# A two-layer adaLN kernel on one core: setup's waits moved into attention, a router in three stages, one product of the slots on VectorE

## The reference

```python
mod = (silu(c) @ wmod).reshape(16, 6, 1, -1)       # sa, ca, ga, sb, cb, gb
ga = (2 * (ga >= 0) - 1) * max(abs(ga), 0.25)       # gb likewise
h = layernorm(x) * (1 + ca) + sa
x = x + ga * mixer(h)       # layer 0: 8-head retention; layer 1: selective scan
h = layernorm(x) * (1 + cb) + sb
x = x + gb * experts(h)     # layer 0: each expert takes its 64 best tokens; layer 1: below

# experts of layer 1
var = mean(x * x, -1)
h = rms_weight * (x * rsqrt(var + 1e-6))
scores = softmax(h @ gate_w.T)                      # 8 experts
top_w, top_i = top_k(scores, 2); top_w /= sum(top_w)
a, g = h @ w1[e].T, h @ w3[e].T
return x + sum over the two e of top_w * ((silu(a) * g) @ w2[e].T)
```

## Time and profile before

| what | us |
|---|---|
| median of 3 runs (lowest, highest) | 1334.08 (1330.05, 1343.19) |
| the profiled execution | 1332.48 |
| its span, first to last instruction | 1330.7 |
| busy in the span: PE, DVE, ACT, POOL | 1047.5, 843.9, 667.6, 621.0 |
| setup to attention's first statistics | 0 to 28.47 |
| router, from its first statistics | 933.89 to 1011.70 |
| slots | 1011.70 to 1049.9 |
| MoE | 1049.9 to 1289.9 |

### The profile page before, as it was taken

The page is one execution under the profiler, slowest core; times in us unless marked ns, Lnnn a source line. Parts: engine busy times, 40 slices in busy tenths (PEclk is TensorE's granted clock), DMA queues, the critical chain, the costliest instruction groups (busy, mean ns, idle before and its releaser), DMA issues. The chain is left out here.

```text
span 1330.7 us, 24554 instructions
## 1 busy us (share of the span) xinstructions
PE 1047.5 (79%) x7112; PEld 826.9 (62%) x7113; DVE 843.9 (63%) x1612; ACT 667.6 (50%) x1488; POOL 621.0 (47%) x922
## 2 busy tenths in 40 slices
PE   1899964899986889998888999861563499999950
PEld 1577752377685788888778888861342277777640
DVE  2566646422234899999999999990577543433327
ACT  1454521433404888888888888840341233333320
POOL 1000001200012899999999999960001456666630
PEclk9988856899997999999999999995665599999985
DMA  6000000375512000000000000005110011111125
GB/s 200 1 1 1 1 1 6 80 167 135 124 33 76 13 13 21 15 12 12 12 12 12 23 13 12 12 1 185 29 32 16 10 39 43 43 41 43 40 80 167
DMA packets 51468, 59.07 MB, mean 44 GB/s; under 512 B 5401, under 2 KB 45282, under 8 KB 50034
## 3 DMA queue, kind: packets, MB, share of 16 engines
q1 hardware_dynamic: 42322, 41.50, 11.8%
q0 software_dynamic: 4608, 9.45, 2.5%
q10 hardware_dynamic: 4496, 7.60, 1.7%
HBM read 49.32 MB, written 9.21 MB: 44 GB/s over the span
## 5 line engine op out<-in xcount | busy, mean ns | idle before, releaser
L1180 DVE TENSOR_TENSOR_SCAN s_hs<-s_dA,bank 128x1024 f32<-128x1024 f32 x128 | 291.6, 2278 | 10.3 <-PE bank L1577 9.6
L1437 POOL TENSOR_SCALAR s_dbuT<-s_dtuT,s_BT 128x256 f32<-128x256 f32 x512 | 241.0, 491 | 11.5 <-POOL s_bc L1375 5.4
L1298 ACT ACTIVATE s_dA<-s_dt,aneg 128x255 f32<-128x255 f32 x512 | 211.7, 495 | 0.2
L1577 PE MATMUL bank<-const,s_dbuT 128*128 128x128 f32 x1024 | 136.1, 277 | 3.1 <-POOL s_dbuT L1437 3.1
L1191 DVE TENSOR_TENSOR s_hc<-s_hs,bank 128x1024 f32<-128x1024 f32 (+1 forms) x128 | 130.3, 1018 | 5.8 <-PE bank L1565 1.1
L1595 PE MATMUL bank<-const,s_hc 128*128 128x128 f32 x832 | 113.9, 276 | 20.9 <-DVE s_hc L1191 20.9
L2102 PE MATMUL bank<-w,x_xT 128*128 x288 | 125.2, 557 | 5.8 <-issue 4.0
L1577 PEld LDWEIGHTS bank<-const,s_dbuT 128*128 128x128 f32 x1024 | 117.0, 143 | 6.3 <-POOL s_dbuT L1437 3.6
L1595 PEld LDWEIGHTS bank<-const,s_hc 128*128 128x128 f32 x832 | 95.5, 142 | 24.7 <-DVE s_hc L1191 24.7
L2140 ACT ACTIVATE x_a<-bank 128x448 f32<-128x448 f32 x72 | 39.1, 544 | 138.5 <-PE bank L2102 138.5
L2062 POOL DMA_INDIRECT x_xg<-hf_rows,x_src x72 | 69.7, 968 | 70.1 <-DVE x_src L2160 40.1
(11 more groups left out here) (298 smaller groups left out, 2198.0 us busy)
## 6 DMA issues: line engine op xcount, KB each, us to landing
xn<-prob_d SPq DMA_DIRECT2D x16, 512.0 KB, 7.5
s_Crow<-C_rows SPq DMA_DIRECT2D x48, 128.0 KB, 2.8
w<-in_w SPq DMA_DIRECT2D x16, 256.0 KB, 3.1
o_yr<-y_rows SPq DMA_DIRECT2D x8, 512.0 KB, 3.9
w<-in_w ACTq DMA_DIRECT2D x1, 3584.0 KB, 13.2
x_res<-in_x SPq DMA_DIRECT2D x4, 512.0 KB
gate<-gates_d SPq DMA_DIRECT2D x2, 1024.0 KB, 5.6
spread<-place_d SPq DMA_DIRECT2D x8, 256.0 KB, 5.8
```

The source lines that it names most:

```text
L1180: dve.tensor_tensor_scan(flat(hs[:, j % 2]), flat(dA[:, j % RING]), bDbu[j % 2], 0.0, ALU.mult, ALU.add).then_inc(S["scanned"], 1)
L1298: ins = act.activation(dA[:, j % RING, h, n, 1:], dt[:, k, h, 1:], ACT.Exp, scale=m.aneg[:, h, 2 * j + n:2 * j + n + 1])
L1437: ins = pool.tensor_scalar(dbuT[:, j % RING, c, n, :], dtuT[:, k, c, :], BT[:, k, c, 2 * j + n:2 * j + n + 1], 1.0, ALU.mult, ALU.mult)
L1577: mm = pe.transpose(out[:, h, n, c * P:(c + 1) * P], dbuT[:, j % RING, c, n, h * P:(h + 1) * P], ident)
```

## The change

- **Setup** ends when the first x load, the front part of `const` (up to `C_T72`, that is without the later tables and the masks), `wq`, `wk`, `wv` and the modulation are there. `wq` to `gn` are issued by ScalarE behind its Silu, and so is the store of `gates`. Everything else stays under way, on six new semaphores `m.late` that live through layer 0. TensorE waits for `wmod` alone and makes the rows of both layers before the columns; VectorE makes `gates` first and `modT` behind them.
- **Attention** waits where each is first used: x pairs 2 and 3, x pairs 4 to 7, the masks, the output weights, the gate rows (at the first gated add, not at the start), layer 1's weights on GpSimd and in ScalarE's fourth round (`growth`).
- **Router**: three stages. n0 takes statistics on VectorE; n1 is normalised on ScalarE, turned, modulated, squared; TensorE takes logits from the modulated rows with `gw`, the router weights times the RMS weight, and mean squares as four 128x8 products; n2 scales the logits and the stored rows by the inverse RMS (4 values a row) on VectorE. `hf` and the second turn are gone; the x add is on GpSimd; rows and three banks are doubled.
- **Slots**: as the stored rows lack the RMS weight, GpSimd multiplies all of `w13` by it, in one instruction at the start of the phase. Its eight products of `hot_hi` move to VectorE, with the tile numbers in bf16.

The diff, cut to its core (VectorE's work on `gates` and `modT` in setup is the same instructions in the other order; the router's helpers that are not shown hold the instructions of before with these waits):

```diff
-        SMALL = [(m.wq, d["wqT"]), (m.wk, d["wkT"]), (m.wv, d["wvT"]), (m.wo, d["woT"]), (m.gate0, d["gate0"]),
-                 (m.gn, d["gn"]), (m.w_in, d["winT"]), (m.bcol, d["cols"]), (m.gate1, d["gate1T"]),
-                 (m.w_outT, d["woutT"]), (m.wdt[32:32 + RDT + 1, :], d["wdtT"]),
-                 (m.taps, d["taps"].partition_broadcast(P).rearrange("p k c -> p (k c)"))]
+        FIRST = [(m.wq, d["wqT"]), (m.wk, d["wkT"]), (m.wv, d["wvT"])]
+        LATER = [(m.wo, d["woT"]), (m.gate0, d["gate0"]), (m.gn, d["gn"])]
+        LAST = [(m.w_in, d["winT"]), (m.bcol, d["cols"]),
+                (m.taps, d["taps"].partition_broadcast(P).rearrange("p k c -> p (k c)")), (m.gate1, d["gate1T"]),
+                (m.w_outT, d["woutT"]), (m.wdt[32:32 + RDT + 1, :], d["wdtT"])]
 
         @block.sync
...
-            sp.dma_start(m.gates_d[:, :], m.gates[:].rearrange("b l g -> b (l g)")).then_inc(s_kept, 16)
-            sp.wait_ge(s_kept, 16)
-            sp.wait_ge(s_x, 16 * (len(BIG) + len(SMALL)))
+            sp.dma_start(*BIG[0]).then_inc(s_x, 16)
+            sp.dma_start(m.const[:, 0:C_T72], d["const"][:, 0:C_T72]).then_inc(s_x, 16)
+            sp.dma_start(*BIG[1]).then_inc(m.late["x1"], 16)
+            sp.dma_start(m.const[:, C_T72:], d["const"][:, C_T72:]).then_inc(m.late["masks"], 16)
+            for i in (2, 3):
+                sp.dma_start(*BIG[i]).then_inc(m.late["x2"], 16)
+            for dst, src in LAST:
+                sp.dma_start(dst, src).then_inc(m.late["layer1"], 16)
+            sp.wait_ge(s_x, 32)
 
         @block.scalar
         def _(act):
...
             act.activation(m.silu_c[:], cT[:], ACT.Silu).then_inc(s_sc, 1)
+            for dst, src in FIRST:
+                act.dma_start(dst, src).then_inc(s_wx, 16)
+            for dst, src in LATER:
+                act.dma_start(dst, src).then_inc(m.late["output"], 16)
+            act.wait_ge(s_gates, 1)
+            act.dma_start(m.gates_d[:, :], m.gates[:].rearrange("b l g -> b (l g)")).then_inc(m.late["gates"], 16)
+            act.wait_ge(s_wx, 16 * len(FIRST))
...
             pe.wait_ge(s_sc, 1)
...
+            pe.wait_ge(s_w, 16)
+
+            def rows(ly):
                 for k, w in enumerate((2, 5)):
...
+                mm.then_inc(s_row, 1)
+
+            def columns(ly):
+                for k, w in enumerate((0, 1, 3, 4)):
...
+            rows(0)
+            rows(1)
+            columns(0)
+            columns(1)
...
             tick(dve.memset(m.ones128[:], 1.0 / D))
-            dve.wait_ge(s_mod, 1)
...
+                if isinstance(n, int) and n == 2:
+                    dve.wait_ge(m.late["x1"], 16)
+                if isinstance(n, int) and n == 3:
+                    dve.wait_ge(m.late["x2"], 32)
...
+                if not later(n) and first == 0:
+                    dve.wait_ge(m.late["masks"], 16)
...
+                if not later(n):
+                    dve.wait_ge(m.late["output"], 48)
...
+                if not later(n):
+                    dve.wait_ge(S["gate"], 16)
...
+            sp.wait_ge(m.late["gates"], 16)
...
+            pool.wait_ge(m.late["layer1"], 96)
...
             act.wait_ge(S["v_zero"], 1)
+
+            def growth():
+                act.wait_ge(m.late["layer1"], 96)
+                act.activation(m.aneg[:], m.bcol[:, :, 3:], ACT.Exp).then_inc(S["w_prep"], 1)
 
             def second_norm(n):
...
+                if isinstance(n3, int) and n3 == 0:
+                    growth()
...
+                if not later(n):
+                    pe.wait_ge(m.late["output"], 48)
...
 
-            body(0, 0, None, None)
-            with eng.Fori(0, PAIRS // 2 - 1, 1) as r:
-                body(2 * r + 1, 1, 2 * r, 0)
-                body(2 * r + 2, 0, 2 * r + 1, 1)
-            body(PAIRS - 1, 1, PAIRS - 2, 0)
+            body(0, None, None, 0)
+            body(1, 0, None, 1)
+            with eng.Fori(0, (PAIRS - 2) // 2, 1) as r:
+                for k in range(2):
...
+            def expert_rows(n, w):
+                dve.wait_ge(S["rows_free"], n + 1)
+                dve.tensor_tensor(rows[:, w], quarters(bH[w], D), rrms[:, w].unsqueeze(2).broadcast_to([P, Q, D]), ALU.mult)\
+                    .then_inc(S["rows"], 1)
...
+            def gated(n, w):
+                dve.wait_ge(S["back_ps"], n + 1)
+                dve.wait_ge(S["added"], n + 1)
+                for k in range(2):
+                    dve.tensor_tensor(gh[:, 2 * k:2 * k + 2, :],
+                                      bH[w][:, k * L:(k + 1) * L].rearrange("p (c d) -> p c d", c=NCH),
+                                      gate[:, bass.ds(2 * n + k, 1), :].broadcast_to([P, NCH, D]), ALU.mult)\
+                        .then_inc(S["gh"], 1)
...
+            def body(n0, n1, n2, odd):
+                if n2 is not None:
+                    scaled_logits(n2, odd)
+                    greatest(n2)
+                    gated(n2, odd)
+                if n0 is not None:
+                    statistics(n0)
+                    moments(n0)
+                if n2 is not None:
+                    below_greatest(n2)
+                if n0 is not None:
+                    shifts(n0)
+                if n2 is not None:
+                    two_best(n2)
+                    share(n2)
+                    inverse(n2)
+                    places(n2)
+                    weights(n2)
+                    expert_rows(n2, odd)
+                    experts(n2)
+
+            for _ in range(2):
+                dve.sem_inc(S["rows"], 1)
+            dve.tensor_scalar(gw[:], m.gate1[:, 0:E1], m.gate1[:, E1:E1 + 1], None, ALU.mult).then_inc(S["gw"], 1)
             dve.wait_ge(S["gate"], 16)
             rounds(dve, body)
...
+            def inverse_rms(n, w):
+                act.wait_ge(S["ms_ps"], n + 1)
+                act.wait_ge(S["rows"], n + 1)
+                act.activation(lrms[:], quarters(bM[w], E1)[:, :, 0], ACT.Ln, bias=m.eps[:, 1:2])\
+                   .then_inc(S["lrms"], 1)
+                act.wait_ge(S["lrms"], n + 1)
+                act.activation(rrms[:, w], lrms[:], ACT.Exp, scale=-0.5).then_inc(S["rms"], 1)
+
...
+                act.wait_ge(S["shift"], n + 1)
+                if later(n):
+                    act.wait_ge(S["xT"], n)
+                for q in range(Q):
+                    act.activation(xn[:, q, :], m.x_res[:, n * Q + q, :], ACT.Identity, bias=shift[:, q:q + 1],
+                                   scale=rstd[:, q:q + 1]).then_inc(S["xn"], 1)
...
+            def body(n0, n1, n2, odd):
+                if n1 is not None:
+                    normalise(n1)
+                if n2 is not None:
+                    inverse_rms(n2, odd)
+                if n1 is not None:
+                    modulate(n1)
+                    squares(n1)
+                if n2 is not None:
+                    exponentials(n2)
+                if n0 is not None:
+                    layer_rstd(n0)
 
             rounds(act, body)
             act.wait_ge(S["weights"], 32)
...
+            def body(n0, n1, n2, odd):
+                if n2 is not None:
+                    pool.wait_ge(S["gh"], 2 * n2 + 4)
+                    xs = m.x_res[:, bass.ds(n2 * Q, Q), :]
+                    pool.tensor_tensor(xs, xs, gh[:], ALU.add).then_inc(S["added"], 1)
...
+            pe.wait_ge(S["gw"], 1)
+            hf = hT[:].rearrange("p s t -> p (s t)")
+
+            def turn(n):
+                pe.wait_ge(S["xn"], Q * n + Q)
+                if later(n):
+                    pe.wait_ge(S["h"], 2 * n)
+                for q in range(Q):
+                    mm = pe.transpose(bT[:, q * P:(q + 1) * P], xn[:, q, :], ident)
+                mm.then_inc(S["xT"], 1)
+
+            def mean_squares(n, w):
+                pe.wait_ge(S["sq"], n + 1)
+                for q in range(Q):
+                    mm = pe.matmul(bM[w][:, q * E1:(q + 1) * E1], sq[:, q * P:(q + 1) * P], m.ones128[:, 0:E1],
+                                   start=True, stop=True)
+                mm.then_inc(S["ms_ps"], 1)
+
+            def turn_back(n, w):
+                for q in range(Q):
+                    mm = pe.transpose(bH[w][:, q * D:(q + 1) * D], hf[:, q * P:(q + 1) * P], ident)
+                mm.then_inc(S["back_ps"], 1)
+
+            def logits(n, w):
+                pe.wait_ge(S["h"], 2 * n + 2)
+                pe.wait_ge(S["rows"], n + 1)
+                for q in range(Q):
+                    mm = pe.matmul(bL[w][:, q * E1:(q + 1) * E1], hf[:, q * P:(q + 1) * P], gw[:], start=True, stop=True)
+                mm.then_inc(S["lg_ps"], 1)
+
+            def body(n0, n1, n2, odd):
+                if n1 is not None:
+                    turn(n1)
+                    logits(n1, 1 - odd)
+                    mean_squares(n1, 1 - odd)
+                    turn_back(n1, 1 - odd)
 
...
-            for c in range(SETS):
-                pool.wait_ge(s_same, c + 1)
-                if c >= 2:
```

(67 more changed lines are left out.)

221 lines of the change are left out of this document (79 added, 142 removed).

## The result

The changed kernel took 1319.24 us in the median of 4 runs (1317.84 to 1326.84), beside 1333.98 for the kernel before; the ratio is 0.9888, 95% interval 0.9856 to 0.9919. The forecast was 1314, range 1305 to 1323. The profiled execution took 1318.45 us, span 1316.7, against 1332.48 and 1330.7 before: 14.0 us less, where 19.6 were forecast.

A forecast was written before the change was run, and what follows sets the result against it. No engine was taken as full throughout; setup, router and slots loop, with no full engine, were priced from their timelines. -9.1 + 0.7 - 15.5 + 4.3 = -19.6 from 1332.48 gave 1312.9, 1314.5 against the median, called 1314; range 1305 to 1323.

The forecast's parts named there:

- Setup: Start of the kernel: attention's first statistics at 19.4 us instead of 28.47, so -9.1 us; bounds -12.2 and -6.
- From there to the router: From attention's first statistics to the router's: +0.2 for `aneg` and +0.5 for semaphores and a barrier, together +0.7 us.
- taken as nothing: Attention's start: `wc` on GpSimd, waiting for last loads near 22 us, could hold VectorE's shift due at 21.4; priced at nothing.
- Router: Whole router stage: 62.3 us against 77.8, so -15.5 us, between -19.7 and -7, with rounds taken as 6.6 us.
- TensorE's ring: Router: TensorE's transposes, modulation wait, logits and mean squares per round, 6.7 us at the low clock, 4.5 at the high.
- the ring over ScalarE: Router: four normalisations and inverse RMS on ScalarE, then VectorE from logits to shift, 5.9 us a round.
- the last two rounds with the hand-over behind them: Router's end: two rounds without new pairs but with the same latencies, 9.2 us, then 3.4 to the next phase.
- The fill: Router's start: from its first statistics to the logits of pair 0, 10.1 us.
- VectorE's ring of 6.1: Router: VectorE's 4.8 us of work, the way over ScalarE and hand-overs make 6.1 us a round.
- Slots: Slots phase: eight sets of 2.49 us instead of 2.76 give -2.0; GpSimd's `w13` pass stops VectorE, +6.3; net +4.3 us.
- The signs of being wrong: Slots' first VectorE instruction ending in 0.4 us beside the pass; router ring over 7.5 us; untouched stages changing length.
- The rival of a lower clock: MoE stage: a denser router costs MoE its TensorE clock, its 224 us becoming 224/c, total 1345 at 0.88; chance 0.04.

The follow-up runs named there:

- run 1: Kernel before with the change's setup, attention and late loads, but the old router and slots phase; ratio 0.9923 to the kernel before.
- run 7: Changed kernel with GpSimd's scaling of the convolution's weights (`wc`) waiting for attention's first shift; one profiled execution, no ratio, shift 0.16 us.
- run 9: Changed kernel with the router's squares and the ones they are multiplied with in bf16; ratio 0.9808 to the kernel before, router 57.7 us.
- run 3: Changed kernel without GpSimd's pass over `w13`, the RMS weight being the scale of a ScalarE copy in MoE; ratio 0.9831 to the kernel before, slots 36.07 us.
- run 5: Changed kernel with mean squares of one quarter only, so its weights are wrong; one profiled execution, no ratio, router 57.6 us.
- run 12: Changed kernel with the pass over `w13` on ScalarE in place of GpSimd; one profiled execution, no ratio, slots 36.08 us.
- run 6: Changed kernel with the router's mean squares against 128 columns of ones in place of 8; ratio 0.9887 to the kernel before, router 63.0 us.
- run 11: Changed kernel once more, unchanged, beside the other experiments; 1342.54 us, ratio 0.9882 to the kernel before.

## Why the prediction was right, and where it missed

- **Setup, -9.1 forecast, -9.12 measured**: right in its steps, also alone (run 1). By the trace SyncE's stall set the end of the new start as taken: it ended at 13.87 (13.8 forecast) and the last issue at 16.26 (16.2). No run takes the stall away.
- **From there to the router, +0.7 forecast, +0.84 measured: luck.** The step "taken as nothing" was wrong: `wc` did hold the first shift, for 1.25 us. I had the last loads near 22, behind the shift due at 21.4; they were in at 20.4. Run 7 takes the hold away. That the sum came out all the same shows nothing, for the stretch took from 899.8 us (run 1) to 913.6 (run 9), and 907.8 in the changed kernel's second profile. Most of this lies in attention and the two phases behind it, and goes with the granted clock: from the first statistics to the expert phase's table load it took 216.6 us at 0.84 in run 1, 220.6 at 0.83 in run 3 and 227.6 at 0.80 in run 9, with the same code in all three. The half us given to six more semaphores is shown by no run.
- **Router, -15.5 forecast, -12.4 measured**. The mechanism was right: TensorE's ring, given as 6.7 at the low clock, measured 6.77 in the six rounds from 936.02 to 976.66, and the ring over ScalarE, given as 5.9, showed itself in runs 5 and 9. Of the 3.1 us missing, 1.0 are the six rounds (40.6 for 39.6): I took 6.6, a little under the low clock's 6.7, and the clock stayed on the lower level throughout. The larger part, 1.8, is the last two rounds with the hand-over behind them (10.4 + 4.0 for 9.2 + 3.4). That term took "the same latencies" without a queue in front of them; in those rounds too the inverse RMS waits behind eight logit and eight mean-square matmuls. The fill took 10.4 for 10.1. VectorE's ring of 6.1 was an overestimate: rounds of 5.88 ran.
- **Slots, +4.3 forecast, +3.83 measured**: right in both parts, sets of 2.47 (2.49 forecast) and 6.0 us for the pass (6.3). The edit that the change adds is its worst part. The Trainium skill's rule of an exclusive lock (SBUF — State Buffer, Who interferes with whom) held for 6 us too, as runs 3 and 12 show. By the same section of the Trainium skill, a VectorE instruction with at most one SBUF input, outside the modes that use two ports, does not contend with GpSimd. The trace agrees: the statistics of run 7 took 0.87 us beside `wc`, as in the kernel before without it.
- **MoE, nothing forecast, +2.8 measured** (with the output phase). The rival of a lower clock had the wrong place: the middle of the phase stays at 1.00. The start is longer by 2.1 us, by a long or a short spell at the low clock. Which one a profile gets is not settled by the change alone: of the twelve traces without idle matmuls six had each. I can't name what decides it; the other 0.7 us are open. The Trainium skill (TensorE: Matmul & The Clock Gate, Part 1: The HAM clock gate) says that this start varies from run to run of one kernel. Between variants of this kernel the traces agree with that, but the two traces of the same kernel, 17.72 and 17.7, do not show it.
- **The signs of being wrong**. Two of the three came true by their letter. The first VectorE instruction of slots did take 0.42 us beside the pass, and so did the second; the hold fell on the third, which ended with the pass as forecast. The sign was set too narrowly: it named one instruction, where the first to begin ran through. And a stage that is not touched, MoE, changed its length, for which the sum had no term. The ring did not exceed 7.5, and no engine waited for a late load in attention's first rounds, apart from GpSimd with `wc`.
- **The sum**: -19.6 forecast, -14.0 in the profiles; by the medians -14.7. It fell into the range because setup and slots were right, the stretch between setup and router came out even by luck, and the two misses together, router and MoE, were 5.9 us.

## What to carry over

Before moving work to an idle GpSimd, look at what VectorE does in that time: here a GpSimd pass of 6.8 us cost 6.0, while a column scale in a ScalarE copy that is made anyway cost nothing that shows. Where a stage's clock stood between the two levels, price its TensorE ring at both, and price the last rounds and the hand-over with the same queue as the full rounds: they held the larger part of the miss. Count small float32 matmuls with their weight loads: at the lower clock eight halves of 8 columns took 1.85 us, four in bf16 0.25. Where a hold is taken as nothing because something else is due first, write down by how little: the shift was due 0.6 us ahead of the loads, and the loads came first by 1. And before a term of under 1 us is called confirmed, look at how much its stretch varies between profiles: here it was 14 us.

## What the runs showed of the hardware

- TensorE's granted clock fell from 0.61 to 0.50 with the new router (the old one had 0.56 in run 1), although TensorE was busy for 66% of the stage (43.27 of 65.45 us) and for 62% before (48.49 of 77.81). In stretches of run 6, which differs in the width of the mean-square matmuls alone, it came back to as much as 0.78. So a shorter and denser stage can run at the lower clock; what decides it no run here shows.
- A GpSimd instruction held VectorE ones with two SBUF inputs for as long as 6.24 us (0.28 alone), and for 1.41 us on 4 elements a row (0.16 alone).
- The MoE phase, counted as in the experiments, took 247.9 and 251.3 us in the first two profiles and 265.9 to 274.6 on the three chips of the experiments, whatever the kernel. These are the gate and up matmuls of TensorE from 1060 to 1260 us, first of the changed kernel's first profile, then of run 11 (line, engine, operation, count, busy us, mean ns, idle before and what ended it):

```profile
L2244 PE MATMUL bank<-w,x_xT 128*128 x256 | 109.9, 552 | 4.5 <-issue 4.3
```

```profile
L2244 PE MATMUL bank<-w,x_xT 128*128 x229 | 101.1, 564 | 15.2 <-ACT x_xT L2286 12.5 <-issue 2.5
```

The same kernel did 64 tiles in 200 us there and 57 here, and TensorE waited 12.5 us for turned rows (ScalarE's copy `x_xT`) that it had not waited for. Why they come later on those chips stays open. For this reason phases are set against each other within a set of runs, and totals only as ratios.
